# Padding the hidden activations and small matrices of a four-stage transformer kernel to whole 128-tiles, one product for low, B and C, and a new hand-set order

## What is computed

```python
x = x + mamba(layernorm(x))      # part P, M, D, G, S, Y of the kernel
x = x + fp4_ffn(layernorm(x))    # part R1, first half
x = x + linear_attention(layernorm(x))   # part R1, second half
x = x + fp4_ffn(layernorm(x))    # part R2
# mamba:   u = xn @ w_in;  low, B, C = split(u @ w_x, [64, 80])     (64 + 16 + 16 columns)
#          dt = softplus(low @ w_dt + b_dt) * 0.099 + 0.001
#          h[d, n] = exp(dt[d] * A[d, n]) * h[d, n] + sum_d(dt * A * u) * B[n];  y[d] = sum_n(h[d, n] * C[n]) + Dp * u
# fp4_ffn: h = silu(q(xn) @ q(w_gate).T) * (q(xn) @ q(w_up).T);  out = q(h) @ q(w_down).T   (704 hidden columns)
```

## Time and profile before

| | |
|---|---|
| median of 3 runs | 2687.83 us (2686.10 to 2688.37) |
| profiled execution, its own time | 2692.52 us |
| its span in the trace | 2690.8 us |
| TensorE (PE) busy | 2374.1 us, 88% |
| VectorE (DVE) busy | 2220.2 us, 83% |
| ScalarE (ACT) busy | 1822.3 us, 68% |
| GpSimd (POOL) busy | 1010.1 us, 38% |
| mean granted TensorE clock | 0.947 of full speed |

### The profile page before, as it was taken

How to read it: one execution, slowest core, us unless ns; L and a number is a source line. 1 busy time by engine, 2 the same in 40 slices (tenths; PEclk the granted TensorE clock), 3 DMA queues, 4 the chain that set the end, 5 groups by cost and what they waited for, 6 DMA issues and landing times.

```text
span 2690.8 us, 40656 instructions
## 1 busy us (share of the span) xinstructions
PE 2374.1 (88%) x12908; PEld 1374.2 (51%) x12908; DVE 2220.2 (83%) x4120; ACT 1822.3 (68%) x3677; POOL 1010.1 (38%) x1632
## 2 busy tenths in 40 slices
PE   2559799998989999898999989899998989979897
PEld 1115456464645646464564646456464545646574
DVE  6887888979888897988889798887979888797744
ACT  4667767685776768576676867767686776756342
POOL 3013343434434343443434344343434434343533
PEclk8669999999999999998999999999999999999998
DMA  3432312212131222313122131312213131221000
GB/s 78 113 103 56 87 43 67 74 53 80 42 92 43 67 75 51 81 42 92 42 64 74 51 87 42 93 42 64 73 52 87 42 87 48 63 71 29 5 5 10
DMA packets 104433, 165.96 MB, mean 62 GB/s; under 512 B 15442, under 2 KB 34078, under 8 KB 104222
## 3 DMA queue, kind: packets, MB, share of 16 engines
q1 hardware_dynamic: 104222, 163.37, 22.3%
HBM read 146.55 MB, written 16.78 MB: 61 GB/s over the span
## 4 chain that ended last, share of the span: by engine, by line
PE 57%; DVE 28%; ACT 6%; issue 5%; POOL 2%; DMA 1%; SPq 0%; DVEq 0%; POOLq 0%; ACTq 0%
PE bank L959 13%; PE bank L942 10%; DVE scan_bufs L1248 8%; PE acc_y L907 6%; PE bank L980 4%; DVE scan_bufs L1258 4%; PE bank L939 4%; PE bank L998 4%; PE bank L952 3%; PE bank L986 2%; PE bank L872 2%; DVE f_h_lean L1100 2%; PE bank L1026 1%; PE bank L877 1%; DVE f_h_max L1132 1%
## 5 line engine op out<-in xcount | busy, mean ns | idle before, releaser
L1248 DVE TENSOR_TENSOR_SCAN scan_bufs<-scan_bufs,inp_bank 128x512 f32<-128x512 f32 x512 | 620.2, 1211 | 17.5 <-ACT scan_bufs L639 17.4
L942 PE MATMUL bank<-w_gu,f_xqT 128*128 128x512 f32 x1024 | 494.6, 628 | 5.4 <-ACT f_xqT L700 5.4
L959 PE MATMUL bank<-w_dn,f_hqT 128*128 128x256 f32 (+1 forms) x1536 | 393.3, 399 | 7.2 <-ACT f_hqT L749 7.2
L907 PE MATMUL acc_y<-scan_bufs,sel_y 128*32 128x512 f32 x1024 | 294.8, 659 | 100.8 <-DVE scan_bufs L1258 99.4
L632 ACT ACTIVATE scan_bufs<-scan_bufs,a_rows 128x512 f32<-128x512 f32 x512 | 366.3, 715 | 4.6 <-DMA scan_bufs<-dt_copy 4.6
L572 POOL TENSOR_SCALAR_AFFINE_SELECT masked_scores<-masked_scores 128x512 f32<-128x512 f32 x256 | 176.0, 711 | 462.9 <-ACT masked_scores L700 462.9
L1258 DVE TENSOR_TENSOR scan_bufs<-scan_bufs,c_bank 128x512 f32<-128x512 f32 x512 | 342.9, 670 | 2.0 <-PE c_bank L893 0.3
L959 PEld LDWEIGHTS bank<-w_dn,f_hqT 128*128 128x128 f32 (+1 forms) x1536 | 277.7, 193 | 129.7 <-issue 84.8
L942 PEld LDWEIGHTS bank<-w_gu,f_xqT 128*128 128x128 f32 x1024 | 196.1, 201 | 265.0 <-issue 263.9
L554 POOL TENSOR_TENSOR f_h<-f_h,f_h_inv 128x704 f32<-128x704 f32 x128 | 191.0, 1492 | 360.6 <-DVE f_h_inv L1143 360.6
L639 ACT ACTIVATE scan_bufs<-scan_bufs 128x512 f32<-128x512 f32 x512 | 319.5, 624 | 0.0
(11 more groups left out here) (203 smaller groups left out, 4580.6 us busy)
## 6 DMA issues: line engine op xcount, KB each, us to landing
scan_bufs<-dt_copy SPq DMA_DIRECT2D x512, 256.0 KB, 3.6
xp<-L_attn_a_x SPq DMA_DIRECT2D x16, 512.0 KB, 4.7
dt_copy<-dt SPq DMA_DIRECT2D x32, 256.0 KB, 2.9
out<-x SPq DMA_DIRECT2D x64, 128.0 KB, 3.1
w_attn<-L_attn_b_W_attn SPq DMA_DIRECT2D x1, 768.0 KB
scan_bufs<-L_ffn_w_gate SPq DMA_DIRECT2D x1, 704.0 KB
scan_bufs<-L_ffn_w_up SPq DMA_DIRECT2D x1, 704.0 KB
masked_scores<-L_ffn_w_down SPq DMA_DIRECT2D x1, 704.0 KB
```

What stands on the lines that cost most here:

```text
L907: last = nc.tensor.matmul(acc_y[32 * j:32 * j + 32, :], sel_y[:, q, :], bar[slot][:, h, :], start=(q == 0), stop=(q == 3), tile_position=( ...
L942: last = nc.tensor.matmul(to[:, :], f.xqT[:, k, :], w_gu[:, k, g, lo:hi], start=(k == 0), stop=(k == DH - 1))
L959: last = nc.tensor.matmul(to[:, 0:D], f.hqT[0:n, k, :], w_dn[0:n, k, :], start=(k == 0), stop=(k == FK - 1))
L1248: nc.vector.tensor_tensor_scan(half, half, inp[:, :], 0.0, ALU.mult, ALU.add)\
```

## The change

- h of the feed-forward blocks lies in a buffer of 6 x 128 columns; the last 64 are set to zero once, as are the last 64 rows of w_down's sixth block. `turn_h` then transposes six whole blocks, `down` contracts over six whole blocks, and ScalarE copies hqT1 in one instruction.
- w_x is padded to 128 columns and w_dt to 128 rows, with zeros. `low` is the whole product u @ w_x (64 + 16 + 16 + 32 zero columns). `B` and `C` are one matmul each: `sel_bc` (0 and 1, made from the identity) picks B's or C's columns out of low and repeats each 8 times. They wait for ScalarE's copy of low where they waited for u. `dt0` and `dt1` contract over all 128 rows.
- The P statistics' `p_var` moves from VectorE to GpSimd.
- GpSimd sets 8 more constants ahead of the others, with four more waits for itself.
- Every step gets a new time in `TIMES`; the last batch's R2 tiles are 4 beats apart in the order, not 3.5. `sum` stays one step for two matmuls.

```diff
@@ -33,66 +33,66 @@
-N_SETUP_POOL = 26
+N_SETUP_POOL = 34
...
-LAST_AT = {"R1": (66, 3), "R2": (94.7, 3.5)}
+LAST_AT = {"R1": (66, 3), "R2": (94.7, 4)}
...
-        ("P", "xT0"): 7.745, ("P", "xT1"): 7.841, ("P", "u0"): 9.915, ("P", "u1"): 10.363, ("P", "low"): 13.779,
-        ("P", "B"): 15.3, ("P", "C"): 32.525, ("P", "dt0"): 14.743, ("P", "dt1"): 24.241, ("P", "G"): 31.341,
-        ("G", "sum"): 2.451, ("Y", "turn"): 0.353, ("R1", "turn_x"): 5.529, ("R1", "up0"): 6.639,
-        ("R1", "up1"): 6.884, ("R1", "turn_h"): 10.005, ("R1", "down"): 10.964, ("R1", "a_turn"): 14.114,
-        ("R1", "a_qkv"): 15.019, ("R1", "a_s0"): 17.41, ("R1", "a_s1"): 17.557, ("R1", "a_sum"): 19.545,
-        ("R1", "a_flip"): 20.108, ("R1", "a_turn_y"): 21.66, ("R1", "a_proj"): 22.725, ("R2", "turn_x"): 4.648,
-        ("R2", "up0"): 6.653, ("R2", "up1"): 7.171, ("R2", "turn_h"): 10.778, ("R2", "down"): 11.833,
+        ("P", "xT0"): 6.582, ("P", "xT1"): 7.599, ("P", "u0"): 10.031, ("P", "u1"): 10.446, ("P", "low"): 14.303,
+        ("P", "B"): 16.386, ("P", "C"): 32.628, ("P", "dt0"): 15.895, ("P", "dt1"): 21.667, ("P", "G"): 30.055,
+        ("G", "sum"): 2.525, ("Y", "turn"): 0.381, ("R1", "turn_x"): 6.111, ("R1", "up0"): 7.485,
+        ("R1", "up1"): 7.543, ("R1", "turn_h"): 11.077, ("R1", "down"): 11.934, ("R1", "a_turn"): 14.92,
+        ("R1", "a_qkv"): 15.756, ("R1", "a_s0"): 18.254, ("R1", "a_s1"): 18.351, ("R1", "a_sum"): 20.554,
+        ("R1", "a_flip"): 21.736, ("R1", "a_turn_y"): 23.523, ("R1", "a_proj"): 23.747, ("R2", "turn_x"): 5.276,
+        ("R2", "up0"): 6.686, ("R2", "up1"): 7.986, ("R2", "turn_h"): 11.363, ("R2", "down"): 12.398,
...
-        ("P", "inp"): 31.364, ("M", "scan"): -0.407, ("M", "read"): 0.308, ("S", "skip"): -0.748,
-        ("Y", "finish"): 0.538, ("R1", "a_qkv"): 16.061, ("R2", "down"): 11.895, ("P", "stats"): 5.451,
+        ("P", "inp"): 31.612, ("M", "scan"): -0.043, ("M", "read"): 0.79, ("S", "skip"): -0.187,
+        ("Y", "finish"): 0.73, ("R1", "a_qkv"): 16.905, ("R2", "down"): 12.9, ("P", "stats"): 4.678,
...
@@ -216,14 +216,14 @@
-        w_x = sb("w_x", [P, DH, RANK + 2 * NS])
-        w_dt = sb("w_dt", [RANK, D])
+        w_x = sb("w_x", [P, DH, P])
+        w_dt = sb("w_dt", [P, D])
...
-        w_xB, w_xC = sb("w_xB", [P, DH, P]), sb("w_xC", [P, DH, P])
+        sel_bc = sb("sel_bc", [P, 2, P])
...
@@ -496,6 +497,17 @@
             setup(pool.memset(sel_y[:, :, :], 0.0))
+            for f in (f1, f2):
+                for wide in f.h_wide:
+                    setup(pool.memset(wide[:, F:FK * P], 0.0))
+            pool.wait_ge(s_set[0], done[0])
+            setup(pool.memset(w_dn[F - (FK - 1) * P:P, FK - 1, :], 0.0))
+            pool.wait_ge(s_set[0], done[0])
+            pool.wait_ge(s_set[0], done[0])
+            setup(pool.memset(w_dt[RANK:P, :], 0.0))
+            pool.wait_ge(s_set[0], done[0])
+            for k in range(DH):
+                setup(pool.memset(w_x[:, k, RANK + 2 * NS:P], 0.0))
...
                 if s == "rstd":
+                    pool.wait_ge(p_mv_ready, upto(b, 1, 0))
+                    pool.tensor_tensor(p_var[:, :], p_mv[:, :, 1], eps_col[:, :].broadcast_to([P, TILES]), ALU.add)\
+                        .then_inc(p_var_ready, 1)
...
@@ -743,10 +758,7 @@
-                    src, done = wait_filled(act, f.part, b, t, "hqT1")
-                    nc.scalar.activation(hqT[:, 3 * P:5 * P], src[:, 0:2 * P], ACT.Copy)
-                    rest = F - 5 * P
-                    nc.scalar.activation(hqT[0:rest, 5 * P:6 * P], src[0:rest, 2 * P:3 * P], ACT.Copy).then_inc(done, 1)
+                    copy_out(f, b, t, "hqT1", hqT[:, 3 * P:6 * P], 3 * P)
...
@@ -865,16 +877,18 @@
-                elif step in ("low", "B"):
-                    w, n = {"low": (w_x[:, :, 0:RANK], RANK), "B": (w_xB, P)}[step]
+                elif step == "low":
                     to, done = take("P", b, 0, step, ["u0", "u1"])
                     for k in range(DH):
-                        last = nc.tensor.matmul(to[0:n, :], w[:, k, :], u[par][:, k, :],
+                        last = nc.tensor.matmul(to[:, :], w_x[:, k, :], u[par][:, k, :],
                                                 start=(k == 0), stop=(k == DH - 1))
+                elif step == "B":
+                    to, done = take("P", b, 0, step, ["low"])
+                    last = nc.tensor.matmul(to[:, :], sel_bc[:, 0, :], low[:, :], start=True, stop=True)
...
-                    last = nc.tensor.matmul(to[:, :], w_dt[:, h * P:(h + 1) * P], dt_low[:, :],
+                    last = nc.tensor.matmul(to[:, :], w_dt[:, h * P:(h + 1) * P], low[:, :],
...
-                wait_drained(pe, "P", b, 0, "u1")
+                wait_drained(pe, "P", b, 0, "low")
...
-                for k in range(DH):
-                    last = nc.tensor.matmul(c_rep[:, :], w_xC[:, k, :], u[par][:, k, :],
-                                            start=(k == 0), stop=(k == DH - 1))
-                last.then_inc(c_ready, 1)
+                nc.tensor.matmul(c_rep[:, :], sel_bc[:, 1, :], low[:, :], start=True, stop=True).then_inc(c_ready, 1)
...
@@ -948,15 +959,13 @@
-                            n = min(P, F - lo)
-                            last = nc.tensor.transpose(to[0:n, k * P:(k + 1) * P], f.h[r][:, lo:lo + n],
+                            last = nc.tensor.transpose(to[:, k * P:(k + 1) * P], f.h_wide[r][:, lo:lo + P],
...
-                        n = min(P, F - k * P)
-                        last = nc.tensor.matmul(to[:, 0:D], f.hqT[0:n, k, :], w_dn[0:n, k, :],
+                        last = nc.tensor.matmul(to[:, 0:D], f.hqT[:, k, :], w_dn[:, k, :],
...
@@ -1209,9 +1219,6 @@
-                    dve.wait_ge(p_mv_ready, upto(b, 1, 0))
-                    nc.vector.tensor_scalar(p_var[:, :], p_mv[:, :, 1], LN_EPS, None, ALU.add)\
-                        .then_inc(p_var_ready, 1)
```

More of the change, by code:

```diff
@@ L35 @@
 HALVES = NS * DH
-N_SETUP_POOL = 26
+N_SETUP_POOL = 34
 PARTS_AT = {"P": (0, 0, 1), "M": (32, 1, 32), "D": (32, 2, 16), "G": (32, 2, 16), "S": (48.95, 16, 2), "Y": (65.0, 1, 2), "R1": (66, 3, 4), "R2": (95.7, 7, 4)}
-LAST_AT = {"R1": (66, 3), "R2": (94.7, 3.5)}
+LAST_AT = {"R1": (66, 3), "R2": (94.7, 4)}
 TIMES = {
     "sp": {
-        ("P", "load"): -3.406, ("P", "keep0"): 14.981, ("P", "keep1"): 27.058, ("D", "spread"): -15.115,
-        ("R2", "down"): 9.437,
+        ("P", "load"): -2.277, ("P", "keep0"): 18.739, ("P", "keep1"): 31.476, ("D", "spread"): -12.121,
+        ("R2", "down"): 8.754,
     },
     "pe": {
[7 rows of a table removed]
[7 rows of a table added]
     },
     "act": {
[13 rows of a table removed]
[13 rows of a table added]
     },
     "dve": {
[14 rows of a table removed]
[14 rows of a table added]
     },
     "pool": {
[5 rows of a table removed]
[5 rows of a table added]
     },
@@ L244, in build @@
         u = [sb(f"u{i}", [P, DH, T]) for i in range(2)]
-        dt_low = sb("dt_low", [RANK, T])
+        low = sb("low", [P, T])
         sp_pos = [sb(f"sp_pos{h}", [P, T]) for h in range(DH)]
@@ L298, in __init__ @@
                 self.part, self.norm = part, Norm(name)
-                self.x, self.h = two("x", [P, D]), two("h", [P, F])
+                self.x, self.h_wide = two("x", [P, D]), two("h", [P, FK * P])
+                self.h = [wide[:, 0:F] for wide in self.h_wide]
                 self.x_max, self.x_scale, self.x_inv = (two(n, [P, D // QB]) for n in ("x_max", "x_scale", "x_inv"))
@@ L402, in _ @@
                 (w_in[:, :, :], w_in_d.rearrange("(k p) e -> p k e", p=P)),
-                (w_x[:, :, :], w_x_d.rearrange("(k p) e -> p k e", p=P)),
-                (w_dt[:, :], w_dt_d),
+                (w_x[:, :, 0:RANK + 2 * NS], w_x_d.rearrange("(k p) e -> p k e", p=P)),
+                (w_dt[0:RANK, :], w_dt_d),
                 (b_dt[:, :], b_dt_d.rearrange("(h p) -> p h", p=P)),
@@ L578, in part_p @@
                 if s == "rstd":
+                    pool.wait_ge(p_mv_ready, upto(b, 1, 0))
+                    pool.tensor_tensor(p_var[:, :], p_mv[:, :, 1], eps_col[:, :].broadcast_to([P, TILES]), ALU.add)\
+                        .then_inc(p_var_ready, 1)
+                    pool.tensor_tensor(p_below[:, :], p_mv[:, :, 0], minus_one[:, :].broadcast_to([P, TILES]), ALU.mult)
                     pool.wait_ge(p_var_ready, upto(b, 1, 0))
[L580 removed]
                     pool.tensor_tensor(p_rstd[:, :], p_var[:, :], minus_half[:, :], ALU.pow).then_inc(p_rstd_ready, 1)
@@ L661, in part_p @@
                 elif step == "low":
-                    evac(step, dt_low[:, :], RANK)
+                    evac(step, low[:, :])
                 elif step == "B":
@@ L1089, in _ @@
                                         a_neg[:, k, :].unsqueeze(2).broadcast_to([P, NS, 8]), -1.0, None, ALU.mult)
-                for w, lo in ((w_xB, RANK), (w_xC, RANK + NS)):
-                    nc.vector.tensor_copy(w[:, k, :].rearrange("p (s d) -> p s d", s=NS),
```

(5 more changed lines are left out.)

1 line of the change is left out of this document (removed), and 60 rows, old and new, of the table TIMES.

## The result

The changed kernel takes 2519.89 us (median of four runs, 2516.88 to 2520.68) against 2687.66 before: a ratio of 0.937, 95% interval 0.936 to 0.939, or 168 us less. The profiled execution took 2520.5 us, its span 2518.8.

The account below looks back on a forecast made before the run. TensorE was taken to bound two thirds of a batch; 57.7 (padding) + 27.5 (single B, C) + 11 (order) = 96 us, 86 counted, took 2692.5 to 2606, less 4.7 for the median: 2601 us. Range 2560 to 2650.

Parts of the forecast that it names:

- How a shape costs time: On TensorE, each change from one shape of weights to another costs 0.14 to 0.20 us.
- few rows cost nothing: Rival, 5%: the surcharge behind a down comes from where it ends, so padding keeps it; 2650 or 2660 us.
- the transposes change shape too: Rival, 2%: turn_h's transposes also pay for their shape, so padding them saves 24 us more; 2577 us.
- the structure: What TensorE computes, without the order: padding 57.7 us and single B and C products 27.5, nine tenths counted, 77 us.
- The h part: Sixth block of down made whole on TensorE: 24.3 us inside and 19.3 behind, together 43.6 us.
- The P part: In part P on TensorE: dt with 128 rows 9.1 us, low with 128 columns 5.0, single B and C 27.5.
- I let nine tenths count: Of the 96 us by which TensorE's list gets shorter, 86 us were taken as saved time.
- VectorE becomes the bound: Rival, 15%: half of TensorE's saving turns into waits for VectorE, 48 us are left; 2640 us.
- New order: it moves waits, and no row gives a price … I take 0: New step times on all engines: waits counted at 0; best end 32 us from earlier statistics of P.
- 60 changes of shape for 11 us: On TensorE, the new order has 716 shape changes instead of 776, at 0.18 us each.
- The slower rival: 6%: sums stand 0.41 beats nearer to the reads they need, so TensorE waits 212 us against 96 saved; 2804 us.
- The head gets shorter: Rival, 15%: all 96 us count, plus 32 from P's earlier statistics at the start of a batch; 2560 us.

Follow-up runs that it names:

- e1: Changed kernel with all step times of the kernel before, the last batch's offsets too: 2645.73 us (0.985 of the kernel before).
- e3: Changed kernel with the padding of h undone (turn_h, its copies and down with 64 rows in the sixth block): 2549.47 us.
- e4: Changed kernel with the old low, B, C and dt of part P, new step times kept: 2553.55 us.
- e7: Changed kernel with the six steps of P from stats to xT1 back at their old times: 2568.93 us.
- e8: Changed kernel in the old order, with a_s1 moved right behind a_s0 so that all 64 pairs stand together: 2655.20 us.
- e9: Changed kernel in the old order, with P's six steps from stats to xT1 and ScalarE's two copies behind the transposes at new times: 2686.19 us.
- e11: Changed kernel in the old order, with decay, square, scan and read at their later new times, sums unmoved: 2809.38 us.
- e13: Changed kernel in the old order, with VectorE's seven steps from gate0 to inv_h of R2 at their new times: 2751.20 us.

## Why the forecast was right in direction and short in size

- **How a shape costs time: right.** e1's TensorE is 5.2 us a batch less occupied, 5.3 were counted. The rival "few rows cost nothing" falls with e3, where a `down` lasts 2.92 us again and the kernel 30 us longer, and so does "the transposes change shape too": `turn_h` kept its 0.11 us each. The Trainium skill's rule in "TensorE: Matmul & The Clock Gate", Why this matters for your kernels, is that a single matmul with few contraction rows takes as long as one with 128. The records of single matmuls agree (after, 128 columns each: 283 ns with 32 rows in line 1007, 277 with 128 rows in line 989), but by it the padding would give nothing, and e3 shows that it gives 30 us in this stream.
- **The size of the structure: too high.** The h part was 43.6 us, 39 at nine tenths; e3 shows 30. The P part was 41.6, 37 at nine tenths; e4 shows 34. "I let nine tenths count" is the term at fault: 77 of 85.3 us, where 67 came in the new order and 40 in the old one, in which TensorE's idle time grew by 2.4 us a batch. By its size that is the rival "VectorE becomes the bound" (2640, and e1 took 2646), but not by its mechanism: of the 2.4 us, 0.9 end with VectorE's work (its sums with x and its reads), and the larger part with ScalarE's copies of h (0.8) and GpSimd's multiplies (0.9).
- **The failed step is "New order: it moves waits, and no row gives a price … I take 0".** It measured 99 us alone and 126 with the structure; the best end that was kept was 32. Four parts of it were in the trace of before and not read as costs. VectorE's instructions with two SBUF operands run up to more than twice as long beside GpSimd (a `dt` sum 1.58 us before, 0.69 after): 31 us. The head of P, counted only by the instructions that move: 49 us by e7, because a second wait of TensorE also costs it its clock. The attention scores that stand apart: 26 us of TensorE's occupied time. And waits inside the gates, 156.0 us for `tanh` before against 33.2 after, which no single move could buy. These overlap and don't add up to 126; how the whole divides stays open, since e8, e9, e11 and e13, each with one group moved, all lose.
- **60 changes of shape for 11 us: too small.** 0.18 us is the mean price of the changes that padding removes. 16 score matmuls by themselves take 1.16 us and 32 in a row 1.72, so a pair put together saves 0.60, and their group is occupied 26 us less. e8 shows that in the old order even this saving was not free to take.
- **The slower rival: a true mechanism, not this case's.** e11 makes it cost 164 us. In the new order the sums wait 110.6 us for the reads against 99.4 before, though the distance got shorter as computed; which of the other moves averts it is not shown.
- **The head gets shorter: right, and still too small.** From the sum ahead of `C` to the first transpose of P, the distance that the prediction named as this rival's sign, a batch takes 21.5 us after and 25.1 before (mean of ten), so 3.6 us. The statistics start 14.9 us behind `inp` and not 18.2, 3.3 us sooner where 2.1 were counted. Even with all of its 32 us this rival ended at 2560. VectorE's busy time as a constant 135 us was wrong: it is 129.2.
- **The direction was not luck:** the structure alone is 40 us faster and the order alone 99. But the larger part of the gain came from a term put at 0.
